# Three graph attention layers on one core: part of x loaded and measured first, four blocks of the second chunk summed in the count stage, three blocks moved to GpSimd, last sums read from PSUM

## The reference

```
h = max(layernorm(x), 0)
x = x + gat(relu(gat(h, W1, 128->256)), W2, 256->128)      # layers 1 and 2
h = max(layernorm(x), 0)
x = x + gat(h, W3, 128->128)                               # layer 3 (denominator + 1e-16)

gat:  f = h @ W;  s = f @ a_src;  d = f @ a_dst
      e = leaky_relu(s[src] + d[dst], 0.2)                 # per edge
      e = exp(e - segment_max(e, dst)[dst])
      out = segment_sum(e * f[src], dst) / segment_sum(e, dst) + b
```

## Time and profile before

| | us |
|---|---|
| median of three runs | 682.75 |
| profiled execution | 681.87 |
| its span | 680.1 |
| PE busy | 591.7 (87%) |
| DVE busy | 637.0 (94%) |
| ACT busy | 483.2 (71%) |
| POOL busy | 459.4 (68%) |

### The profile page before, as it was taken

How to read it: one execution, slowest core, us unless ns; L and a number is a source line. 1 busy time by engine, 2 the same in 40 slices (tenths; PEclk the granted TensorE clock), 3 DMA queues, 4 the chain that set the end, 5 groups by cost and what they waited for, 6 DMA issues and landing times.

```text
span 680.1 us, 13823 instructions
## 1 busy us (share of the span) xinstructions
PE 591.7 (87%) x5571; PEld 574.7 (84%) x5571; DVE 637.0 (94%) x911; ACT 483.2 (71%) x719; POOL 459.4 (68%) x448
## 2 busy tenths in 40 slices
PE   1729855899979899999999999999989989999995
PEld 1628755799969799899989989898988989999994
DVE  3999999999999989999987999999998899999994
ACT  0416545556969778887666796979886699788891
POOL 5579101779928565775954685859698679596883
PEclk9978988799989999999999999999999999999998
DMA  2410002000000000000100100000010010010001
GB/s 73 118 55 2 1 8 15 25 2 1 20 1 1 20 1 20 1 2 8 28 12 1 27 1 21 1 19 1 8 21 19 1 27 12 29 33 7 20 1 42
DMA packets 22325, 12.07 MB, mean 18 GB/s; under 512 B 12393, under 2 KB 20055, under 8 KB 22255
## 3 DMA queue, kind: packets, MB, share of 16 engines
q1 hardware_dynamic: 21455, 9.85, 6.3%
q0 software_dynamic: 800, 1.26, 0.6%
HBM read 9.47 MB, written 1.64 MB: 16 GB/s over the span
## 4 chain that ended last, share of the span: by engine, by line
DVE 54%; PE 22%; issue 9%; DMA 5%; ACT 4%; POOL 4%; POOLq 0%; DVEq 0%
DVE scratch L952 21%; DVE ps L1068 17%; PE ps L1814 16%; DVE scratch L1150 6%; DMA xr<-in_x 3%; DVE ps L1070 2%; POOL scratch L752 2%; ACT scratch L1568 2%; ACT scratch L1570 2%; DVE ps L1080 1%; PE ps L1867 1%; PE ps L1845 1%; PE ps L1781 1%; DVE scratch L1068 1%; DMA gathered<-in_edges,start_i 1%
## 5 line engine op out<-in xcount | busy, mean ns | idle before, releaser
L1814 PE MATMUL ps<-hB,scratch 125*125 125x129 f32 x3450 | 403.9, 275 | 19.8 <-DVE scratch L1150 15.5
L1814 PEld LDWEIGHTS ps<-hB,scratch 125*125 125x125 f32 x3450 | 388.6, 187 | 28.6 <-DVE scratch L1150 21.2
L752 POOL TENSOR_TENSOR scratch<-scratch,C 125x625 f32<-125x625 f32 x239 | 303.9, 1283 | 110.9 <-ACT scratch L1570 108.9
L1068 DVE SCALAR_TENSOR_TENSOR ps<-C,a_unit,ps 125x625 f32<-125x625 fp8e3 x330 | 275.9, 867 | 2.3
L1568 ACT ACTIVATE scratch<-gathered,r_neg 125x625 f32<-125x625 f32 x219 | 176.4, 806 | 15.4 <-PE ps L1814 14.4
L1570 ACT ACTIVATE scratch<-scratch,r_src 125x625 f32<-125x625 f32 x219 | 178.9, 817 | 7.1
L1453 ACT ACTIVATE C<-ps 125x1000 fp8e3<-125x1000 f32 x80 | 78.3, 1000 | 77.2 <-PE ps L1781 77.2
L1781 PE MATMUL ps<-scratch 128*125 128x125 bf16 x1250 | 95.0, 241 | 32.0 <-DVE scratch L952 30.5
L1781 PEld LDWEIGHTS ps<-scratch 128*125 128x125 bf16 x1250 | 90.5, 156 | 35.8 <-DVE scratch L952 33.4
L1150 DVE SCALAR_TENSOR_TENSOR scratch<-ps,r_src,C 125x625 f32<-125x625 f32 x121 | 104.3, 862 | 5.1 <-PE ps L1804 5.1
L952 DVE TENSOR_TENSOR scratch<-key_lo,ps 128x4000 bf16<-128x4000 bf16 (+3 forms) x41 | 87.6, 2136 | 0.4 <-PE ps L1781 0.3
(11 more groups left out here) (195 smaller groups left out, 450.9 us busy)
## 6 DMA issues: line engine op xcount, KB each, us to landing
gathered<-g_lines SPq DMA_DIRECT2D x15, 305.2 KB
xr<-in_x SPq DMA_DIRECT2D x1, 1562.5 KB
...
```

The source lines that it names most:

```text
L752: g.tensor_tensor(slot[s], slot[s], C5[:, q % NC, s, :], ALU.mult).then_inc(pool_done, 1)
L1068: v.scalar_tensor_tensor(dest, counts, unit[:, s:s + 1], top, ALU.min, ALU.max).then_inc(S.top_done, 1)
L1814: last = mm(ps[0:P, acc_at(t):acc_at(t) + HW], A[:, P * t:P * (t + 1)], feat, start=opens and t in (0, 3), stop=closes, skip_group_check=True)
```

## The change

1. *Start.* The first ten tiles of x are loaded right after the sample, ahead of the weights, and the rest, with the two broadcast biases b2r and b3r, after the first edge window. DVE computes the statistics of those ten tiles before it waits for the window (`first_statistics`), and of the other 15 where all 25 were.
2. *Count stage.* `SECOND` = 4: blocks (1,0) to (1,3) are summed in it, made by POOL alone, 29 blocks in 14 tiles. The row maxima ahead of chunk 1 are now those of s = 4 to 9.
3. *Chunks 1 and 2.* DVE's own blocks of chunk 1 go from (17, 19, 21, 23) to (20, 22), of chunk 2 from nine to six; fewer tops of later chunks lie in chunk 1; the follow-up parts stand at later steps.
4. *`ALONE`.* Blocks 7, 10, 15 and 18 of layer 1's chunks are made by POOL alone where they are not already POOL's. In chunks 2 and 3 they are all POOL's, and chunk 1 is excluded; in chunk 4 three of them, 7, 10 and 18, were DVE's.
5. *Tail.* `last_result` reads the sums in PSUM (`acc3`) instead of ACT's copy, which is left out; the transposes of the last chunk's tops stand three blocks earlier.

```diff
-        OWN = ((), (17, 19, 21, 23), (1, 4, 7, 10, 13, 15, 18, 20, 22), (1, 5, 9, 13, 16, 19, 22), (0, 2, 4, 7, 10, 12, 14, 16, 18, 20, 22))
+        OWN = ((), (20, 22), (2, 5, 8, 12, 17, 20), (1, 5, 9, 13, 16, 19, 22), (0, 2, 4, 7, 10, 12, 14, 16, 18, 20, 22))
 
         KEYS_TILE = 4
+        X_FIRST = 10
         FEAT_AT = tuple(KEYS_TILE + 2 + r for r in range(len(FEATS)))
         EXT_AT = FEAT_AT[-1] + 3
         OVER_AT = EXT_AT + 2
         EXPS_AT = OVER_AT + 1
-        SECOND = 0
+        SECOND = 4
...
-                       At(16, (17, 17, 18, 18), 18, (19, 19, 20), None, (24,), (23, 25, 29), (25, 27, 31), 27, 29),
-                       At(10, (11, 11, 12, 12), 12, (13, 13, 14), None, (20,), (17, 20, 25), (19, 22, 27), 22, 24),
+                       At(20, (21, 21, 22, 22), 22, (23, 23, 24), None, (24,), (27, 29, 32), (29, 31, 34), 31, 33),
+                       At(12, (13, 13, 14, 14), 14, (15, 15, 16), None, (21,), (19, 22, 27), (21, 24, 29), 24, 26),
...
-                      spread_tops(0, AHEAD, T, 0, 13) + spread_tops(1, 0, 10, 14, 25) + spread_tops(1, 10, 14, AFTER, AFTER),
-                      spread_tops(1, 14, T, 0, 10) + spread_tops(2, 0, 17, 10, 25) + spread_tops(2, 17, 21, AFTER, AFTER),
+                      spread_tops(0, AHEAD, T, 0, 13) + spread_tops(1, 0, 7, 14, 25) + spread_tops(1, 7, 9, AFTER, AFTER),
+                      spread_tops(1, 9, T, 0, 12) + spread_tops(2, 0, 16, 12, 25) + spread_tops(2, 16, 21, AFTER, AFTER),
                       spread_tops(2, 21, T, 0, 4) + spread_tops(3, 0, T, 4, 24) + spread_tops(4, 0, AHEAD, AFTER, AFTER))
...
-        POOL_OF = tuple(pool_tiles(q) for q in range(Q))
+        ALONE = ((7, 10, 15, 18), (), ())
+
+        def alone(q):
+            return tuple(s for s in ALONE[q // NC] if s not in pool_tiles(q)) if q > 1 and not turn(q) else ()
+
+        POOL_OF = tuple(tuple(sorted(pool_tiles(q) + alone(q))) for q in range(Q))
         FIRST_OWN = {q: {min(s for s in range(t, T) if s not in POOL_OF[q]): t for t in (0, EARLY_TILES, LATE)}
                      for q in range(NC, Q, NC)}
         def post_at(q):
...
-            return q == 0 and not (s % 4 == 3 and s < 16) or q == 1 and s < SECOND
+            return q == 0 and not (s % 4 == 3 and s < 16) or q == 1 and s < SECOND or s in alone(q)
...
         @block.sync
         def _(sp):
             sp.dma_start(sample_i[:, :], apart[0, :, :]).then_inc(edges_in, 16)
+            sp.dma_start(xr[:, 0:X_FIRST, :], x_v[:, 0:X_FIRST, :]).then_inc(x_in, 16)
             sp.dma_start(w1[:, :], W1).then_inc(weights_in, 16)
             sp.dma_start(w2[:, :, 0:D], W2.rearrange("(k p) f -> p k f", p=128)).then_inc(weights_in, 16)
             sp.dma_start(w3[:, 0:D], W3).then_inc(weights_in, 16)
@@ -508,12 +515,13 @@
             for v, pair in ((av2, (a_src2, a_dst2)), (av3, (a_src3, a_dst3))):
                 for i, a in enumerate(pair):
                     sp.dma_start(v[:, i:i + 1], a.unsqueeze(1)).then_inc(weights_in, 16)
-            sp.dma_start(b2r[:, :], b2.unsqueeze(0).broadcast_to([P, D])).then_inc(weights_in, 16)
-            sp.dma_start(b3r[:, :], b3.unsqueeze(0).broadcast_to([P, D])).then_inc(weights_in, 16)
             sp.wait_ge(first_in, 16)
-            sp.dma_start(xr[:, :, :], x_v).then_inc(x_in, 16)
+            sp.wait_ge(x_in, 16)
+            sp.dma_start(xr[:, X_FIRST:T, :], x_v[:, X_FIRST:T, :]).then_inc(x_in, 16)
+            sp.dma_start(b2r[:, :], b2.unsqueeze(0).broadcast_to([P, D])).then_inc(x_in, 16)
+            sp.dma_start(b3r[:, :], b3.unsqueeze(0).broadcast_to([P, D])).then_inc(x_in, 16)
             sp.wait_ge(gather_in, 16 * (WG - 1))
-            sp.wait_ge(x_in, 16)
+            sp.wait_ge(x_in, 64)
             sp.dma_start(edge_sb[:, :, :], edges.rearrange("(p k) c -> p k c", p=P)).then_inc(edges_in, 16)
             sp.wait_ge(edges_in, 32)
...
-                if s == 0:
+                if s == min(p for p in POOL_OF[q] if by_pool(q, p)):
                     pool.wait_ge(ga_loaded, 16 * (q + 1))
                 if n >= RING and n != T - 1:
                     pool.wait_ge(F.pe_done, slot_free(n))
-                g.tensor_scalar(slot[s], ga[q], LARGEST, r_src[0][:, s:s + 1], ALU.min, ALU.max).then_inc(first_max, 1)
+                g.tensor_scalar(slot[s], ga[q % 2], LARGEST, r_src[q // NC % 2][:, s:s + 1], ALU.min, ALU.max).then_inc(first_max, 1)
 
...
             def node_statistics():
+                dve.wait_ge(x_in, 64)
+                for t in range(X_FIRST, T):
+                    last = v.bn_stats(bn6[:, t, :], xr[:, t, :])
+                last.then_inc(F.ln_lin, 1)
+                dve.wait_ge(F.ln_lin, 2)
+                for t in range(X_FIRST, T):
+                    last = v.bn_aggr(mv[:, t, :], bn6[:, t, :])
+                last.then_inc(F.ln_stats, 1)
+
+            def first_statistics():
                 dve.wait_ge(x_in, 16)
-                for t in range(T):
+                for t in range(X_FIRST):
                     last = v.bn_stats(bn6[:, t, :], xr[:, t, :])
                 last.then_inc(F.ln_lin, 1)
                 dve.wait_ge(F.ln_lin, 1)
-                for t in range(T):
-                    last = v.bn_aggr(mv[:, t, :], bn6[:, t, :])
-                last.then_inc(F.ln_stats, 1)
+                for t in range(X_FIRST):
+                    v.bn_aggr(mv[:, t, :], bn6[:, t, :])
 
...
                           hB[:, 0:COLS * LANES // 2]).then_inc(iota_copied, 1)
+            first_statistics()
             dve.wait_ge(first_in, 16)
             first_keys()
...
                     if h == 0:
-                        dve.wait_ge(raw_half, Q)
+                        dve.wait_ge(acc_half, Q)
                     else:
-                        dve.wait_ge(F.raw_ready, Q)
-                    v.tensor_tensor(z0, raw[:, t0:t1, D], scale, ALU.mult).then_inc(F.z_lin, 1)
+                        dve.wait_ge(F.pe_done, Q * T)
+                    v.tensor_tensor(z0, acc3[h][:, :, D], scale, ALU.mult).then_inc(F.z_lin, 1)
                     dve.wait_ge(F.z_lin, n + 1)
                     v.tensor_scalar(z, z0, HALVED * 1e-16, None, ALU.add).then_inc(F.z_lin, 1)
                     dve.wait_ge(F.z_lin, n + 2)
@@ -1242,7 +1260,7 @@
                     dve.wait_ge(F.rz_ready, Q + h)
                     for t in range(t0, t1):
                         xt = xr[:, (NC - 1) * CT + t, :]
-                        last = v.scalar_tensor_tensor(xt, raw[:, t, 0:D], rz[:, t:t + 1], xt, ALU.mult, ALU.add)
+                        last = v.scalar_tensor_tensor(xt, acc3[h][:, t - t0, 0:D], rz[:, t:t + 1], xt, ALU.mult, ALU.add)
                     last.then_inc(y_ready, 1)
 
             set_mode(0)
...
-            move_sums(Q - 1, True)
 
             def exps(A, B, a, al, out_sem):
...
                     elif s == T - 1:
-                        if q == Q - 1:
-                            top_transpose(F, q)
                         last_products(q)
+                    if q == Q - 1 and s == T - 4:
+                        top_transpose(F, q)
                     if q:
                         if s == post_at(q).tops:
```

More of the change, by code:

```diff
@@ L355, in gat_stack_kernel @@
         K = Steps(*(sem("careful_" + name) for name in Steps._fields))
-        N_WEIGHTS, N_CONSTS, KEY_STEPS = 15, 8, 9
+        N_WEIGHTS, N_CONSTS, KEY_STEPS = 13, 8, 9
         LAYERS = 3
@@ L1137, in aggregate @@
             def aggregate(S, q):
-                dve.wait_ge(S.ln_lin, q % NC + 2)
+                dve.wait_ge(S.ln_lin, q % NC + (3 if S is F else 2))
                 for t in range(CT):
@@ L1623, in chunk @@
                         for p in POOL_OF[i] if i < Q else ():
-                            if pass_at(i, p) == q * T + s:
+                            if pass_at(i, p) == q * T + s and not by_pool(i, p):
                                 row_maximum(i, p)
```

2 lines of the change are left out of this document (1 added, 1 removed).

## The result

| | before | changed |
|---|---|---|
| median (8 runs each) | 682.33 us (681.57 to 683.83) | 685.31 us (682.97 to 687.22) |
| ratio, 95% interval | | 1.0046 (1.0032 to 1.0059) |
| span of the profiled execution | 680.1 | 683.4 |
| clock granted to PE, mean over the span | 0.972 | 0.960 |

The change makes the kernel 3.1 us slower, by its ratio; 680.6 was forecast, with a range to 684.5. Slower had a chance of 0.22. The changed kernel's runs also lie further apart, 4.2 us against 2.3.

The account below looks back on a forecast made before the run. The span was taken as mostly DVE's (54% of the chain, PE 22%), with PE fuller in chunk 2. Terms -3.0 +1.0 -2.3 +0.95 +2.6 -1.4 = -2.15 gave 679.7 against 681.87, 680.6 us as a median; range 675 to 684.5.

Parts of the forecast that it names:

- the one for chunk 1: Chunk 1: DVE's chain of maxima sets the end, PE waits for (1,20); end at 233.2 against 235.49, -2.3 us.
- Start: Start: ten tiles' statistics and aggregations move into DVE's idle stretch, and a 0.34 wait goes; -3.0 us.
- Rival C: Start: loading x first delays the first gather or weights by 3 us, so -3.0 turns to 0; 683.6; chance 0.14.
- Count stage: Count stage: the extra blocks overrun at tile 22 (+0.5) and in a hand-off at the end (0.5); +1.0 us.
- Rival B: End of count stage: POOL's 3.09 wait returns in full, stage ends 4.1 later instead of 1.0; 683.7 us; chance 0.20.
- Chunk 4: Chunk 4: blocks 7 and 10 on POOL delay block (4,11), for which PE waits; +2.6 us.
- Rival D: Chunk 4: the blocks by POOL alone cost nothing; -4.75, 678.0 us; chance included in the forecast case's 0.44.
- Chunks 2 and 3: Chunks 2 and 3: +0.5 in chunk 2 from more waits, 0.45 of moved-up posts returning in chunk 3; +0.95 us.
- Tail: Tail: transposes three blocks earlier and no ACT copy in between bring DVE's last result forward; -1.4 us.
- Rival A: Whole kernel: every hand-off holds, PE's four blocks less come out in full; -8.5, 674.3 us; chance 0.22.

Follow-up runs that it names:

- experiment 7: Changed kernel with PE multiplying by zeros before its waits for blocks (1,20), (1,24) and (4,11): 682.71 us, 1.0000.
- Experiment 9: Block (1,24) ahead of the scaling on POOL: on experiment 6, 678.95 us, 0.9949; with product (1,20) also right behind DVE's join, 677.45 us, 0.9931.
- experiment 1: Kernel before with the start's part alone (ten tiles of x and their statistics first): 680.7 us, 0.9969.
- experiment 6: Changed kernel without `ALONE`, the three chunk 4 blocks by POOL alone: 682.31 us, 0.9995.

## Why the prediction was wrong

**The step that failed** is the one for chunk 1: "Before, 235.49. So -2.3, not -4.4", and under it the sentence that stood for every term, "I keep the clock of the trace of before throughout". The wait itself was forecast well: "PE ... is done at 218.4 to 218.9 and waits", product (1,20) "ready at about 223.5". In the trace PE was done at 217.5 and the product came at 222.1, 1.8 earlier as everything there, so 219.3 and 223.9. What was not priced is what a wait of over four us does to the clock. In the same count the transposes, forecast to end near 225.3, ended at 227.6 (225.76 in the trace); `rz`, forecast for 229.0, came at 231.3; and the end of the chunk, 233.2, at 237.3.

Kept busy in experiment 7, PE went through chunk 1 in 33.95 us instead of 36.14, where the forecast comes to 32.5 (34.79 before, less 2.3). So 2.2 of these 3.6 us were the clock. The rest is not: product (1,20) came 0.4 later than forecast, and the last products, put at 1.6, take 2.4 at the full clock too (before, 233.13 to 235.49).

The sum also took over POOL's order, "with block (1,24) behind it (1.25), as before". POOL stood idle for 10.34 us ahead of `rz`, not for about 4, while the row maximum of this block was ready at 219.43. Experiment 9 shows what that order cost.

**The reading behind it.** The trace of before told of the clock in the count stage, where PE waits before every tile (timeline of PE, 32 matmuls a tile):

```profile
109.84 3.59 PE L1781 MATMUL ps<-scratch 128*125 128x125 bf16 x32 [3.45 <-DVE scratch L952]
...
118.43 2.15 PE L1781 MATMUL ps<-scratch 128*125 128x125 bf16 x32 [2.15 <-DVE scratch L952]
```

The granted clock of the two is 0.53 and 1.00; at the slow tile of the earlier trace rows, behind a wait of 1.12, it is 0.53. The first here has a wait near the one forecast for chunk 1, and its tile was slow. I took the lower clock for a matter of the count stage ("if a tile of the count stage runs at the lower clock in the new order"), and looked for it in no rival. The changed kernel made PE's work in chunk 1 shorter while DVE's stayed; that turns work into idle time, and idle time is not free on PE.

**Start**: direction right, -3.0 against -1.64. DVE's key step started when forecast (39.92 against 39.8), but took 2.42 us, not 1.19. I checked only that POOL's L680 had room for the gain, and not what POOL does beside this step once it comes earlier. The earlier trace rows has the wait of 3.08 but not POOL's product from 38.68 to 41.06, which lies there in the trace of before. Rival C was a small part: the first window landed 0.46 later in the changed kernel and 1.2 in experiment 1, without moving the end of the key step in the latter.

**Count stage**: +1.0 against -0.16 in one pair of traces, some +0.7 over all traces, so the forecast stands about as well as the single reading. Rival B did not come. POOL's last block of chunk 0 ended at 175.29, before at 180.40: 5.1 earlier, of which 1.6 is the start's and 3.1 the wait that went, as forecast. The overrun at tile 22 did not come, since its count ran at the full clock (2.15, before 3.54), which was luck; PE's wait of 0.65 for block (1,1) lies ahead of a longer one for DVE (1.45 at 193.66), so that DVE and not PE set the end of the stage.

**Chunk 4**: mechanism right, term too small, +2.6 against +4.04: the wait was 2.96 (forecast 2.7), and the clock took about 1.4 more (experiment 7). Some 0.5 is there without the three blocks too (35.55 against 35.00 in experiment 6). Rival D fell.

**Chunks 2 and 3**: +0.77 against +0.95, but the parts are other ones: 0.1 in chunk 2, where 0.5 was given to waits, and 0.66 in chunk 3, where 0.45 was expected. That the sum fits is in part luck.

**Tail**: -1.44 against -1.4, as forecast, and the results take as long from PSUM as from scratch.

**Rival A** had at most a part of the truth. With POOL's order changed, chunk 1 is 1.7 us shorter with the four blocks than without (33.00 against 34.71), of its 4.4, and the whole time shows nothing of it (0.9949 against 0.9952).
